# Block-transposed softmax normalisation, ScalarE-issued rows of maxima and 96+1-row weight loads in a MetaFormer kernel

## The reference

```
x = x + windowed_attention(ln(x))        # 12 heads of 16, windows of 14x14, relative positions
t = t + W_out @ gelu(W_in @ ln(t))       # 192 -> 768 -> 192
x = x + spectral_mix(ln(x))              # 2-D FFT per image, complex 2-layer map, inverse, plus a dense bias path
t = t + mixture_of_experts(ln(t))        # 8 experts, top 2, 192 -> 768 -> 192
```

## Time and profile before

| what | value |
|---|---|
| median of 3 runs | 738.89 us (737.77 to 743.34) |
| profiled execution, its own time | 742.52 us |
| its span in the trace | 740.7 us |
| mean granted PE clock | 0.842 of full |
| busy in the span | PE 625.7, PEld 503.3, DVE 327.9, ACT 220.7, POOL 134.6 us |
| start up to the first attention pair | 0 to about 132 us |
| attention pairs 0 to 5 | about 132 to 312 us |
| rest (projection, feed-forward, mixing, experts) | about 312 to 740.7 us |

### The profile page before, as it was taken

The page is one execution under the profiler, slowest core; times in us unless marked ns, Lnnn a source line. Parts: engine busy times, 40 slices in busy tenths (PEclk is TensorE's granted clock), DMA queues, the critical chain, the costliest instruction groups (busy, mean ns, idle before and its releaser), DMA issues.

```text
span 740.7 us, 13578 instructions
## 1 busy us (share of the span) xinstructions
PE 625.7 (84%) x4592; PEld 503.3 (68%) x4593; DVE 327.9 (44%) x946; ACT 220.7 (30%) x554; POOL 134.6 (18%) x113
## 2 busy tenths in 40 slices
PE   0499999999779698799999998987249999999992
PEld 0377886756547465566666886966249999999991
DVE  4344435458567564571112263535603334443431
ACT  1012322324233223322223142141114444444440
POOL 6020100510000000000000004224313333333332
PEclk9989965557686655799999999988569999999997
DMA  2722585835163371077000001003122233323221
GB/s 83 162 65 59 155 198 111 189 96 82 27 97 59 46 110 35 10 268 308 1 0 1 1 1 44 16 28 124 59 61 39 43 44 45 45 43 43 43 38 17
DMA packets 32969, 53.63 MB, mean 72 GB/s; under 512 B 6458, under 2 KB 26484, under 8 KB 31410
## 3 DMA queue, kind: packets, MB, share of 16 engines
q1 hardware_dynamic: 24962, 43.51, 24.7%
q0 software_dynamic: 7968, 9.60, 7.6%
HBM read 32.95 MB, written 20.29 MB: 72 GB/s over the span
## 4 chain that ended last, share of the span: by engine, by line
PE 68%; SPq 8%; DVE 8%; DMA 6%; issue 4%; ACT 2%; POOL 2%; DVEq 0%; ACTq 0%; POOLq 0%
PE ps L1631 10%; PE ps L1617 7%; PE ps L1622 5%; PE ps L1462 4%; PE ps L1324 4%; PE ps L1184 4%; PE ps L1185 3%; PE ps L1450 3%; PE ps L1315 3%; DMA x<-in_xp 3%; PE ps L1519 2%; PE ps L1361 2%; PE ps L1604 2%; POOL xs_d L552 2%; PE ps L1454 2%
## 5 line engine op out<-in xcount | busy, mean ns | idle before, releaser
L565 POOL DMA_INDIRECT out<-ys,place_i x39 | 66.9, 1715 | 125.3 <-DVE ys L1161 70.9
L1631 PE MATMUL ps<-w2e,hts 128*128 x468 | 82.7, 327 | 1.5 <-DVE ys L1161 1.5
L1631 PEld LDWEIGHTS ps<-w2e,hts 128*128 128x128 f32 x468 | 75.1, 190 | 1.9 <-issue 1.8
L1324 PE MATMUL ps<-qa,ka 48*98 48x196 f32 x384 | 61.6, 457 | 8.1 <-ACT pt L634 5.9
L552 POOL DMA_INDIRECT xs_d<-rows,slot_i x32 | 31.5, 986 | 190.6 <-DVE slot_i L1073 182.0
L871 DVE TENSOR_REDUCE negm<-ps 98x2 f32<-98x392 f32 x96 | 49.1, 553 | 37.9 <-PE ps L1279 37.7
L741 ACT ACTIVATE hts<-ps,wst 128x128 f32<-128x128 f32 x234 | 64.5, 382 | 2.2 <-PE ps L1622 2.2
L634 ACT ACTIVATE pt<-ps 98x392 f32<-98x392 f32 x96 | 42.5, 494 | 66.7 <-PE ps L1324 66.7
L1617 PE MATMUL ps<-xst,wst 128*128 128x128 f32 x468 | 60.0, 279 | 1.1 <-ACT xst L574 1.1
L1617 PEld LDWEIGHTS ps<-xst,wst 128*128 128x128 f32 x468 | 58.4, 195 | 1.7 <-issue 1.7
L879 DVE RECIPROCAL rsum<-ps 128x128 f32<-128x128 f32 x48 | 42.3, 923 | 30.3 <-PE ps L1361 30.3
(11 more groups left out here) (212 smaller groups left out, 1024.6 us busy)
## 6 DMA issues: line engine op xcount, KB each, us to landing
w1e<-in_w1e SPq DMA_DIRECT2D x8, 579.0 KB, 10.2
w2e<-in_w2e SPq DMA_DIRECT2D x8, 576.0 KB, 11.1
xs<-xs_d SPq DMA_DIRECT2D x39, 98.0 KB, 1.9
ka<-k_d SPq DMA_DIRECT2D x12, 170.0 KB
k_d<-kst SPq DMA_DIRECT2D x16, 121.5 KB, 1.9
x<-in_xp SPq DMA_DIRECT2D x4, 384.0 KB, 20.2
q_d<-qt SPq DMA_DIRECT2D x2, 768.0 KB, 5.5
qa<-q_d SPq DMA_DIRECT2D x12, 128.0 KB
```

What stands on the lines that cost most here:

```text
L565: nc.gpsimd.indirect_dma_start(acc, bass.IndirectOffsetOnAxis(ap=place_i[:, j % 2:j % 2 + 1], axis=0), ys[:, j % 2, :], None, compute_op=A ...
L1324: last = mm(ps[0:98, banks[e], k * WIN:(k + 1) * WIN], ka[head(e), n, key_cols(b) + 98 * k:key_cols(b) + 98 * k + 98], qa[head(e), n, b * ...
L1631: last = mm(ps[:, 5, 0:D], hts[:, u, k, :], w2e[:, ds(e, 1), k, :], start=(k == 0), stop=(k == HT - 1))
```

## The change

1. **Normalisation.** `invert` and `outputs` are replaced by `sums_out(p, k, step)` with four steps: a 32x32 block transpose of the product bank from PSUM into `ott`; a reciprocal of one column in each block (128x16 elements); a multiplication of the 16 output columns of each block by it (128x256 elements) into `onr`; a block transpose of `onr` into `ot`. Each step waits for the one before it. For half 1 of pair p-1 the steps stand ahead of maxima 2, 3, 4 and 5. PE's wait ahead of product 0 of pair p is no longer for `o_ok` (the whole normalisation) but for `o_tr` (the first transpose). A memset of `onr` is added once.
2. **Rows of maxima.** SP's `max_rows` is gone; ACT issues the same four DMAs in `turn_max`, behind its two copies and a wait for them, ahead of exponential 14 of the running pair.
3. **PE's order and waits.** The waits for `lf`, `m_in` and `v_pair` move from the start of the pair to behind maximum units 0 and 1 and behind `product(p-1, 4)`, which moves ahead of the scores of step 0. The wait for `lb` stays first.
4. **Weights.** `wqkv` (on SP's queue), `wproj` and `wb` (on POOL's) are each sent as 96 partitions and 1.

```diff
-            sp.dma_start(wqkv[:], a["wqkv"]).then_inc(s["w1_in"], 16)
+            sp.dma_start(wqkv[0:C], a["wqkv"][0:C]).then_inc(s["w1_in"], 16)
+            sp.dma_start(wqkv[C:C + 1], a["wqkv"][C:C + 1]).then_inc(s["w1_in"], 16)
...
-                if rows:
-                    max_rows(p + 1, 1 - n)
                 sp.wait_ge(s["o_ok"], 1 + 2 * p + 2)
...
-            for dst, name in ((wproj, "wproj"), (win, "win"), (wout, "wout"), (wb, "wb"), (dft, "dft"), (idft, "idft"),
-                              (ab1, "ab1")):
+            for dst, name in ((wproj, "wproj"), (wb, "wb")):
+                nc.gpsimd.dma_start(dst[0:C], a[name][0:C]).then_inc(s["w2_in"], 16)
+                nc.gpsimd.dma_start(dst[C:C + 1], a[name][C:C + 1]).then_inc(s["w2_in"], 16)
+            for dst, name in ((win, "win"), (wout, "wout"), (dft, "dft"), (idft, "idft"), (ab1, "ab1")):
...
                 nc.scalar.activation(erow[:, n, :], ps[0:8, MAX_BANKS[2], 2 * P:3 * P], ACT.Copy).then_inc(s["m_row_ok"], 1)
+                act.wait_ge(s["m_row_ok"], 2 * p + 2)
+                for e in range(2):
+                    r = e * HALF + AUG - 1
+                    row = qa[r:r + 1, n, :].rearrange("o (b t) -> o b t", b=NIMG)[:, :, 0:WIN]
+                    act.dma_start(row, mrow[8 * e:8 * e + 8, n, :]).then_inc(s["m_in"], 16)
+                    row = qa[r:r + 1, n, :].rearrange("o (bp par t) -> o bp par t", bp=NIMG // 2, par=2)
+                    act.dma_start(row[:, :, :, WIN:],
+                                  erow[4 * e:4 * e + 4, n, :].rearrange("p (par t) -> p par t", par=2)[:, :, 4:]
+                                  ).then_inc(s["m_in"], 16)
...
+            def sums_out(p, k, step):
+
+                done = 2 * p + k
+                if step == 0:
                     dve.wait_ge(s["pv"], 1 + 5 * p + (3, 5)[k])
+                    nc.vector.transpose(ott[:], ps[:, 5 + k, :]).then_inc(s["o_tr"], 1)
+                elif step == 1:
+                    dve.wait_ge(s["o_tr"], done + 1)
+                    nc.vector.reciprocal(rinv[:], by_block(ott[:])[:, :, HD]).then_inc(s["o_rec"], 1)
+                elif step == 2:
+                    dve.wait_ge(s["o_rec"], done + 1)
+                    nc.vector.tensor_tensor(by_block(onr[:])[:, :, 0:HD], by_block(ott[:])[:, :, 0:HD],
+                                            rinv[:].unsqueeze(2).broadcast_to([P, 16, HD]), ALU.mult
+                                            ).then_inc(s["o_nrm"], 1)
+                else:
+                    dve.wait_ge(s["o_nrm"], done + 1)
+                    if k == 0:
+                        dve.wait_ge(s["o_out"], 1 + 64 * p)
+                    nc.vector.transpose(ot[:, k, :], onr[:]).then_inc(s["o_ok"], 1)
...
                     if INVERT_AT <= mu < INVERT_AT + 4 and not first:
-                        invert(p - 1, 1, mu - INVERT_AT)
-                    if mu == INVERT_AT + 4 and not first:
-                        outputs(p - 1, 1)
+                        sums_out(p - 1, 1, mu - INVERT_AT)
...
-                pe.wait_ge(s[f"lf{n}"], itp * 128 + 128)
-                pe.wait_ge(s["m_in"], 64 * p + 64)
-                pe.wait_ge(s["v_pair"], 2 * p + 2)
                 if more:
                     pe.wait_ge(s[f"lb{1 - n}"], (itp + n) * 128 + 128)
                 for j in range(10):
...
+                    if j == 0:
+                        if not first:
+                            product(p - 1, 1 - n, 4)
+                        pe.wait_ge(s["v_pair"], 2 * p + 2)
+                        pe.wait_ge(s[f"lf{n}"], itp * 128 + 128)
+                        pe.wait_ge(s["m_in"], 64 * p + 64)
                     score_units(p, n, j)
...
-                            pe.wait_ge(s["o_ok"], 1 + 2 * p)
+                            pe.wait_ge(s["o_tr"], 2 * p)
                         product(p, n, PRODUCT_AT[j])
-                    if j == 0 and not first:
-                        product(p - 1, 1 - n, 4)
```

More of the change, by code:

```diff
@@ L131, in metaformer @@
         ot = sb("ot", [P, 2, 512], stack=att)
-        rsum = sb("rsum", [P, 512], stack=att)
-        carry = sb("carry", [1, 1], stack=att)
+        ott = sb("ott", [P, 512], stack=att)
+        onr = sb("onr", [P, 512], stack=att)
+        rinv = sb("rinv", [P, 16], stack=att)
         att.close()
@@ L225, in metaformer @@
                  "const_in lb0 lb1 lf0 lf1 v_pair "
-                 "m_ps m_red m_turned m_row_ok m_in t_ps t_exp pv o_rec o_shuf o_ok o_out o_last0 o_last1 "
+                 "m_ps m_red m_turned m_row_ok m_in t_ps t_exp pv o_zero o_tr o_rec o_nrm o_ok o_out o_last0 o_last1 "
                  "ao_in p_ps res n4 t4 xt4_ok h_ps h_ok f_ps "
@@ L347, in load_pair @@
                                          rel_d[low][kind][ds(WS * e + 2 * WS * p, WS), :]).then_inc(sq, 16)
[L349 to L359, removed]
             store_rels(0)
@@ L381, in _, with pair_step @@
             store_rels(2)
-            max_rows(0, 0)
             store_rels(3)
             load_pair(1, 1, 0)
-            def pair_step(p, n, more, rows=True):
+            def pair_step(p, n, more):
                 if more:
@@ L531, in _ @@
             nc.gpsimd.dma_start(ab2[:], a["ab2"].broadcast_to([FT, 4 * C])).then_inc(s["w2_in"], 16)
-            pool.wait_ge(s["w2_in"], 16 * 11)
+            pool.wait_ge(s["w2_in"], 16 * 13)
             late_op(nc.gpsimd.tensor_scalar(aw1[:, :, 2, :], aw1[:, :, 1, :], -1.0, None, ALU.mult))
@@ L871, in maxima, with by_block @@
                 nc.vector.tensor_reduce(dst, src, X, ALU.max, negate=True).then_inc(s["m_red"], 1)
-            def invert(p, k, part):
-                if part == 0:
-                    dve.wait_ge(s["pv"], 1 + 5 * p + (3, 5)[k])
[L877 to L890, removed]
+            def by_block(t):
+                return t.rearrange("p (b c) -> p b c", c=32)
+            def sums_out(p, k, step):
+                done = 2 * p + k
+                if step == 0:
+                    dve.wait_ge(s["pv"], 1 + 5 * p + (3, 5)[k])
+                    nc.vector.transpose(ott[:], ps[:, 5 + k, :]).then_inc(s["o_tr"], 1)
[12 more added lines that the diff above has]
+                    nc.vector.transpose(ot[:, k, :], onr[:]).then_inc(s["o_ok"], 1)
             def pair(p, n, first, last):
@@ L895, in pair @@
                     if INVERT_AT <= mu < INVERT_AT + 4 and not first:
-                        invert(p - 1, 1, mu - INVERT_AT)
-                    if mu == INVERT_AT + 4 and not first:
-                        outputs(p - 1, 1)
+                        sums_out(p - 1, 1, mu - INVERT_AT)
                     if not last:
                         maxima(p + 1, 1 - n, mu)
-                for part in range(4):
-                    invert(p, 0, part)
-                outputs(p, 0)
+                for step in range(4):
+                    sums_out(p, 0, step)
+            nc.vector.memset(onr[:], 0.0).then_inc(s["o_zero"], 1)
             for mu in range(20):
                 maxima(0, 0, mu)
+            dve.wait_ge(s["o_zero"], 1)
             relative(3)
@@ L912, in _ @@
             pair(NPAIR - 1, 1, False, True)
-            for part in range(4):
-                invert(NPAIR - 1, 1, part)
-            outputs(NPAIR - 1, 1)
+            for step in range(4):
+                sums_out(NPAIR - 1, 1, step)
             def carry_wait():
@@ L1086, in mixing @@
                 mixed(it)
-            dve.wait_ge(s["w2_in"], 16 * 11)
+            dve.wait_ge(s["w2_in"], 16 * 13)
             dve.wait_ge(s["moe_in"], 16 * 7)
@@ L1221, in _ @@
             turn_image(0, 0, first=True)
-            pe.wait_ge(s["w1_in"], 16)
+            pe.wait_ge(s["w1_in"], 32)
             with pe.Fori(0, NIMG // 2 - 1) as it:
@@ L1417, in turn @@
                 last.then_inc(s["t4"], 1)
-            pe.wait_ge(s["w2_in"], 16 * 11)
+            pe.wait_ge(s["w2_in"], 16 * 13)
             pe.wait_ge(s["ones_ok"], 4)
```

## The result

The changed kernel takes 727.99 us (median of 4 runs, 725.09 to 728.53) against 740.78 (4 runs, 737.77 to 743.34): ratio 0.9852, 95% interval 0.9803 to 0.9901. On another chip the same pair gave 721.92 against 737.79, ratio 0.9801 (0.971 to 0.9891). Executions that are over 1.5% slower than the fastest one of their kernel are left out of the ratios, but not out of the medians and ranges. The profiled execution took 727.59 us (span 725.7), 14.9 less than that of before.

A forecast was written before the change was run, and what follows sets the result against it. Bounds: DMAs of x, of rows of maxima and of the last outputs, then PE from 312 us. Sum: 742.5 - 14.5 - 6 - 2.6 = 719.4, that execution being 3.6 above the median, so 716; range 700 to 731.

The forecast's parts named there:

- Step 1: Start: wqkv sent as 96 rows and 1 uses all 16 engines; 14.5 us less, bounds 12.7 and 15.8.
- Step 2: Attention pairs: ACT's four issues of rows of maxima take 2.7 us; PE loses 2.4, or 1.7 in pairs 0 and 4.
- step 3: Pair starts, SP's chain: pairs 1 to 3 at 27.8 us against 29.86; all pairs 6 less, bounds 14 less, 6 more.
- the 24.9 itself: Attention pairs 1 to 3: own work of 24.9 us, read from 161.07 to 185.95 in pair 1.
- The term beside it: Next pair's first steps: 1 us less for each of three pairs, assuming the clock falls in the idle time.
- 1.7 us more for each of pairs 0 and 4: Pairs 0 and 4: no wait to win back, so each takes 1.7 us more, 3.4 together.
- The last term of the sum: Behind the attention, from 312 us on: PE work on unchanged code, its 428 us carried over.
- Step 4: Normalisation by block transposes: 2.3 us in place of 4.94; 2.6 less at the end of attention, bounds 1.2 and 3.5.
- A: Rival, attention pairs: the clock stays up, saving some 31 us in place of 6, total 691; chance 0.14.
- B: Rival, pairs: clock up in fewer pairs, or ACT's issues dearer; 4 us more, not 6 less, total 726; chance 0.18.
- C: Rival, start: the split doesn't do what it says, 14.5 us don't come, total 730; chance 0.11.
- D: Rival, pairs: ACT's issues held in a busy queue; over 1% slower from 2.1 us an issue, 754 at 2.5; chance 0.05.

The follow-up runs named there:

- kernel 1: The kernel before with only wqkv split into two transfers: 724.29 us against 738.51, ratio 0.9804.
- kernel 10: The changed kernel with wqkv as one transfer of 97 rows again: 738.82 us against 737.79 for the kernel before, ratio 1.0027.
- kernel 3: The changed kernel with the rows of maxima back on SP: 708.34 us against 738.51 for the kernel before, ratio 0.9595.
- the repetition: The changed kernel, unaltered, once more on another chip: 721.92 us against 737.79 for the kernel before.
- kernel 6: kernel 3 with the old normalisation: 726.46 us against 736.75 for the kernel before, ratio 0.9835.
- kernels 8: kernel 3 with the bf16 loads of pair p+3 issued ahead of SP's wait for the outputs: 696.65 us against 736.75 for the kernel before, ratio 0.9427.
- 12: kernel 3 plus one useless copy on ACT ahead of exponential 14: 693.5, 698.26, 700.83 and 725.32 us against 737.79 for the kernel before.

## Why the prediction was wrong

**Step 1 was right.** Forecast 14.5 us, image 2 at 23.6; measured 12.6 to image 2 (23.71), 15.1 to pair 0, 14.2 as a change by itself (kernel 1) and 16.9 in its absence (10), 1.1 above my upper bound. By the Trainium skill, "DMA: Bandwidth & Descriptors", section "Why a DMA increments its semaphore by 16 and not by 1", 97 rows run on one engine and 96 on 16; the trace agrees, with shares of 0.07 and 0.85 to 1.16.

**Step 2 was right in its own terms and wrong in what followed.** I took 2.7 us for the block and 2.4 for PE's loss. Measured are 2.85 for the block, with 0.64 to 0.66 for an issue, and 3.08 of idle time of PE, where kernel 3 has 0.58 at the same place: a loss of 2.5. The Trainium skill, "DMA: Bandwidth & Descriptors", section "Issuing engines are not separate DMA queues", says that issuing from several engines saves only the sequencer's time for the issues. The traces agree: 2.9 us were taken from SP and 2.85 given to ACT; where they land is what mattered.

**The step that failed is the sum of step 3,** "own work 24.9 us, plus 2.4, plus 0.5 of handover, is 27.8". It takes the last steps of a pair at the high clock of the earlier trace rows and adds the stall as a constant. But a stall of 3 us there takes the clock with it: step 9 ran in 1.63 us in place of 0.91 and the last products in 1.53 in place of 0.87, and pairs took 30.97. Two terms of the sum are wrong.

The larger one is missing. PE was busy for 9.62 us of the high stretch before, and for 7.07 of the changed kernel's. So 2.55 us of work moved to the low clock, where it takes about as much again. The other is the 24.9 itself, which starts 1.2 us too late: I read pair 1 from 161.07, but pair 2 from 189.91, its first maximum unit. Pair 1's first maximum unit is in the same timeline of the kernel before:

```profile
159.89 0.54 PE L1279 MATMUL ps<-kb,qb 48*98 48x196 bf16 x4
```

From 159.89 to 185.95 the own work is 26.1 us, and 26.1 + 2.5 + 2.55 is 31.1, an estimate from these rows (without the handover, for which no idle time shows), against the 30.97 measured. Without the clock's term it would be 28.6, against 30.0 for this pair before (189.91 less 159.89).

The term beside it, 1 us gained in each next pair because the idle time at the pair's start was gone, had the wrong sign: the low clock came earlier, not later. I had noted that the clock fell in the idle time before, and not asked whether the idle time that I was adding would do the same. And 1.7 us more for each of pairs 0 and 4 was wrong the other way: there the clock came up, and pair 4 took some 2 us less. Kernel 3's 27.1 us are no confirmation of the 27.8, which had the stall in it: they hold 2.06 us of waiting for the bf16 loads, which I had expected ahead of PE.

In all, the attention part was forecast at 8.6 us less (6 and 2.6), and measured at 3.2 less in the profiled execution and at nothing in kernel 10. Against kernel 1, which has the same start, the changed kernel's trace has 7.8 us less idle time of PE in the attention and 12.0 us more of busy PE, at a clock of 0.67 in place of 0.73. These are two single executions, but they show the exchange. The last term of the sum, no change behind 312 us, was off by 3.3 in the profiled execution, and by 1.4 the other way in the repetition (427.6 against 429.0).

**Step 4 was right:** 0.72, 0.25, 0.42, 0.71, together 2.21 us against 2.3. Its worth inside the pairs was under-sized. I let it act through SP's chain at 2.1 us a pair; kernel 6 against 3 gives 18 us for all of it, where an earlier `o_ok` also keeps the idle time at a pair's start small. That the clock makes the difference is read from the traces (of 21 us between the two in the attention, 16.9 are busy PE; kernel 6 has one low stretch of 81.9 us, up to 160.3, and one of 47.8, where kernel 3's first ends at 127.9 and none is over 13.7 in pairs 1 to 4), not tested by itself.

**The rivals.** A, the clock stays up, did not come, though runs of kernels 8 and 12 reach 693 to 701, its region. The Trainium skill, "TensorE: Matmul & The Clock Gate", section "HAM oscillation — how this bites in real kernels", describes PE waiting for operands, the clock falling, and the next work starting slow each time; the changed kernel's trace agrees in five pairs, with 3.0 to 3.1 us of waiting, for ACT and not for a DMA, just ahead of each fall. B was nearest, by luck: its 726 came from pairs that cost 4 us more in all, where the attention part measured between 3.2 less and 1 more (kernel 10). Nor did its mechanism come: the clock rose in more pairs than before (0 and 4 too), not in fewer, but for 10.2 us in place of 13.7. C and D are refuted by the shares near 1 and the 0.66 us.

## What to carry to other kernels

Here a stall cost its length and then what it did to PE's clock. So price the work behind it at the low clock too, and ask what lies behind it: here a pair with 4 us of idle time at its end took 30.0 us, and one with 3 us ahead of its last steps 30.97. DMA issues on a busy compute engine should stand one by one behind its long instructions, not in a row ahead of one that PE waits for. When a change has several parts, run its cheapest line alone: here the row count of one transfer was the whole gain. The rest only paid once the block on ACT was taken out (708 us), and most once the bf16 loads were ordered by when they are needed (697 us). And count a period from one instruction to the same one of the next round.

## What the runs showed of the hardware

An f32 block transpose of 128x512 from PSUM takes 0.72 us, the same as a stream shuffle of that size, and a reciprocal over 16 columns 0.25 where one over 128 takes 0.92. A DMA issue takes ACT's sequencer 0.65 us, as on SP, but the activation ahead of it keeps running, so a lone issue behind an exponential costs 0.36 us of idle time. The granted clock repeats with the pairs: in all three traces with ACT's block (the changed kernel, its repetition and kernel 10) they have 10.2 us high and 20.5 low. And executions of the same program on one chip lay 17 and 27 us apart (704 and 721; 698 and 725), each time with the lower mean clock in the longer one, so a few runs of such a kernel don't settle 2%.
